# A rarely taken search on VectorE: eight pairs of MAX8 and replacement written out in place of a hardware loop over two pairs

## The chip, the cores and the metric

One core of one Trainium2 chip runs the whole program. The metric is the device time of one execution in microseconds (us), as the median of several runs. Times inside the kernel come from one profiled execution.

## The reference, cut to what matters

A decoder layer runs over 32 sequences of 256 tokens with 512 features: self-attention with 16 heads of 32 features and a gate, then cross-attention, then a mixture of adapter matrices, with a layer norm behind each. The part that matters here is the attention, which keeps for each query and head only the 64 largest of its 256 scores:

```python
scores = jnp.einsum('bhqd,bhkd->bhqk', qn, kn)
temp = jax.nn.sigmoid(x.mean(axis=1) @ Wt + bt) + 0.5
scores = scores / temp[:, None, None, :]
kk = max(1, S // 4)
vals, idx = jax.lax.top_k(scores, kk)
w = jax.nn.softmax(vals, axis=-1)
...
out = jnp.einsum('bhqk,bhkd->bhqd', attn, v)
```

## The kernel before

The work is cut by sequence (called a batch here), and within one by `s`, of which there are four: 128 queries by 8 heads. Every engine has a hand-written order of steps, the function `body`, in which three sequences overlap: the front of sequence i+1, the attention of i and the end of i-1. On PE, ACT and POOL the bodies follow one another as straight code. On VectorE (DVE) two bodies, for an even and an odd sequence, stand inside a hardware loop (lines 2051 to 2054). The loop is run 14 times and covers sequences 2 to 29; sequences 0, 1, 30 and 31 have bodies of their own, so there are six bodies with attention in the code.

Per `s`, the threshold of each row is not found by a full sort. A guess is made from the moments of the row, ACT subtracts it while it copies the scores (`copy_scores`, L789) and counts signs (L809), and DVE looks at the 16 scores nearest to the guess (`search`, L1824 to L1835) and picks the threshold (`set_threshold`). A head in which some row cannot be settled in this way is doubtful. PE and ACT count them, and DVE reads the count into a register in `keep_top` (L1863).

`keep_top` then has two ways. If no head of the eight is doubtful, eight instructions of `keep_above` (L1867) mask the probabilities with the threshold and sum them. Otherwise the code of the `Else` part makes a mask of the doubtful heads in a register and goes through the heads one by one: a settled head gets `keep_above`, a doubtful one gets `keep_struck`, which strikes the eight largest scores of every row eight times over (`strike`: MAX8, L1873, and a replacement, L1874), and keeps what was struck (L1883). Both ways end at the reciprocal `kept_inv` (L1905), for which POOL waits to scale the probabilities (L523) and ACT to copy the next scores into the buffer that comes free (L789).

Each `strike` waits on the semaphore `slow` after both of its instructions. `Steps.restart` (L51 to L56) waits until the count is reached and clears the semaphore. In the kernel before, this is done in every pass of the loop over two strikes. The call site of both ways is:

```python
with dve.If(n < 1):
    for k in range(HS):
        keep_above(k)
with dve.Else():
...
    for k in range(HS):
        step.n = before + k
        with dve.If((doubtful & 2 ** k) > 0):
            keep_struck(k)
```

The `Else` part stands in the code behind the eight `keep_above`, so that the usual way jumps over it (the unconditional branch of L1887).

Of the kernel before, what the change touches and what calls it, by code (L numbers as in the profile page):

```python
# [31 lines left out]
def at(batch, per_batch, n):  # L32

    return batch * per_batch + n
# [24 lines left out]
def decoder_layer(nc, x, ctx, aWq, abq, aWk, abk, aWv, abv, aWo, abo, aWt, abt, aWg, abg,  # L59
# [12 lines left out]
    ROUNDS = KEEP // 8  # L72
# [4 lines left out]
    with stack:  # L77
# [1632 lines left out]
        def _(dve):  # L1710
            step = Steps(dve, s_dve)
            slow = Steps(dve, s_slow)
# [143 lines left out]
            def keep_top(b, s):  # L1856

                r = s % 2
                dve.wait_ge(s_th, at(b, NS, s + 1))
                dve.wait_ge(s_ex, at(b, NS * NH, NH * s + NH))  # L1860
                dve.wait_ge(s_fl, at(b, NS, s + 1))
                dve.sem_inc(s_seq_v, 1)
                n = dve.value_load(unsure_n[0:1, r, HS:HS + 1].bitcast(I32), min_val=0, max_val=MOST)  # L1863
                before = step.n
                def keep_above(k):
                    h, j = divmod(k, HQ)
                    step.mark(dve.scalar_tensor_tensor(  # L1867
                        out=probs[:, r, h, j], in0=scores[:, r, h, j], scalar=threshold[:, r, k:k + 1],
                        in1=probs[:, r, h, j], op0=ALU.is_ge, op1=ALU.mult, accum_out=kept_sum[:, r, k:k + 1]))

                def strike(k):
                    h, j = divmod(k, HQ)
                    slow.wait(slow.mark(dve.max(top8[:], scores[:, r, h, j])))  # L1873
                    slow.wait(slow.mark(dve.match_replace(scores[:, r, h, j], top8[:], scores[:, r, h, j], STRUCK)))  # L1874

                def keep_struck(k):

                    h, j = divmod(k, HQ)
                    with dve.Fori(0, ROUNDS // 2):
                        strike(k)  # L1880
                        strike(k)
                        slow.restart()
                    step.mark(dve.scalar_tensor_tensor(  # L1883
                        out=probs[:, r, h, j], in0=scores[:, r, h, j], scalar=STRUCK / 2,
                        in1=probs[:, r, h, j], op0=ALU.is_le, op1=ALU.mult, accum_out=kept_sum[:, r, k:k + 1]))
# [5 lines that stand above are left out]
                    slow.wait(slow.mark(dve.scalar_tensor_tensor(  # L1891
                        out=head_bits[:, 0:HS], in0=unsure_n[:, r, 0:HS], scalar=0.0, in1=bit_weights[:],
                        op0=ALU.is_gt, op1=ALU.mult, accum_out=head_bits[:, HS:HS + 1])))
                    slow.mark(dve.tensor_copy(head_mask[:], head_bits[:, HS:HS + 1]))
                    slow.restart()
                    doubtful = dve.value_load(head_mask[0:1, 0:1], min_val=0, max_val=2 ** HS - 1)
# [7 lines that stand above are left out]
                step.wait(step.n)  # L1904
                dve.reciprocal(kept_inv[:, r], kept_sum[:, r]).then_inc(s_inv, 1)  # L1905
# [178 lines left out]
```

## Time and profile before

| what | value |
|---|---|
| median of 3 runs | 3202.72 us (3202.55 to 3206.73) |
| profiled execution, its own time | 3211.29 us |
| span of the profiled execution | 3209.3 us |
| DVE busy | 2729.7 us (85%), 10113 instructions |
| PE busy | 2837.4 us (88%) |
| ACT busy | 2119.9 us (66%) |
| POOL busy | 1583.2 us (49%) |
| mean granted clock of PE | 0.959 of full speed |

The time of the profiled execution runs about 2 us beyond its span. Register, branch and semaphore instructions are handled by an engine's sequencer and are not counted as busy; in the trace they stand under the name of the engine with a q (DVEq). An instruction that replaces (MATCH_REPLACE in the program) is recorded as two, MATCH_VALUE_LOAD and MATCH_REPLACE8, and a SCALAR_TENSOR_TENSOR with a sum as two, itself and DVE_READ_ACCUMULATOR. The packets by which instructions are loaded into the engines stand in the DMA part under "instruction".

### The profile page before, as it was taken

The page shows a single profiled execution, that of the slowest core. Times are in us where ns is not written, and L with a number is a line of the kernel's source. Part 1 is how long each engine was busy: PE and PEld are TensorE (multiplying, and loading weights), DVE is VectorE, ACT ScalarE, POOL GpSimd, SP SyncE. Part 2 cuts the span into 40 slices and gives each one's busy share as a digit, 9 for nine tenths or more (in the row PEclk, how much of TensorE's full clock was granted, in tenths as well). Part 3 has the DMA queues.
Part 4 walks back from the last instruction along what each step waited for, and adds up shares of the span by engine and source line. Part 5 has one row for each costly group of instructions (what it writes and reads, how often), then busy time and mean ns, then how long its engine had stood idle before and what let it go on. Part 6 is the DMA issues. An engine that isn't in the chain of part 4 may idle for free. (4 is left out here: it accounts for less than half of the span.)

```text
span 3209.3 us, 58791 instructions
## 1 busy us (share of the span) xinstructions
PE 2837.4 (88%) x16154; PEld 1560.3 (49%) x16154; DVE 2729.7 (85%) x10113; ACT 2119.9 (66%) x5970; POOL 1583.2 (49%) x2285
## 2 busy tenths in 40 slices
PE   6799999989899789998998999999988998989755
PEld 4455555545455345554554555555545554545333
DVE  4889889888888898888888898988988898888881
ACT  3577777766576557766766777777767776657541
POOL 3345555545455444554544554555545454545422
PEclk8899999999999989999999999999999999999877
DMA  6000000000000000000000000000000000000000
GB/s 226 8 18 25 25 24 22 19 10 24 24 25 22 5 24 25 25 22 4 25 25 24 25 21 25 17 13 25 25 24 22 24 18 11 24 24 18 9 10 13
DMA packets 43674, 80.04 MB, mean 25 GB/s; under 512 B 3914, under 2 KB 12106, under 8 KB 43186
## 3 DMA queue, kind: packets, MB, share of 16 engines
q1 hardware_dynamic: 41682, 69.18, 6.6%
q0 software_dynamic: 1504, 5.77, 0.5%
q14 instruction: 354, 2.90, 0.3%
q8 instruction: 134, 2.20, 0.3%
HBM read 58.16 MB, written 16.78 MB: 23 GB/s over the span
## 5 line engine op out<-in xcount | busy, mean ns | idle before, releaser
L523 POOL TENSOR_SCALAR probs<-probs,kept_inv 128x256 f32<-128x256 f32 x1024 | 474.0, 486 | 611.0 <-DVE kept_inv L1905 611.0
L789 ACT ACTIVATE scores<-score_ps,neg_guess 128x256 f32<-128x256 f32 x1024 | 397.5, 480 | 233.4 <-DVE kept_inv L1905 197.8
L1867 DVE SCALAR_TENSOR_TENSOR probs<-scores,threshold,probs 128x256 f32<-128x256 f32 x1011 | 434.0, 492 | 137.5 <-ACT unsure_n L815 107.5
L809 ACT ACTIVATE near<-scores 128x256 f32<-128x256 f32 x1024 | 411.3, 415 | 4.2 <-DVE nearest L1834 1.1
L824 ACT ACTIVATE probsT<-work_ps 128x512 f32<-128x512 f32 x512 | 292.7, 597 | 181.0 <-PE work_ps L1122 178.4
L1830 DVE MATCH_REPLACE8 near<-nearest,near 128x256 f32<-128x256 f32 x1024 | 406.8, 407 | 0.0
L1122 PE MATMUL work_ps<-ident,probs 128*128 128x128 f32 x2072 | 324.0, 291 | 79.2 <-POOL probs L523 36.7
L1826 DVE MAX8 nearest<-near 128x8 f32<-128x256 f32 x1024 | 358.1, 410 | 9.8 <-DVE near L1818 8.7
L1834 DVE MAX8 nearest<-near 128x8 f32<-128x256 f32 x1024 | 356.9, 409 | 0.0
L490 POOL TENSOR_TENSOR inv_norm<-sumsq,minus_half 128x32 f32<-128x32 f32 x64 | 351.2, 5488 | 5.3
L1818 DVE TENSOR_SCALAR near<-scores,flip 128x256 int32<-128x256 int32 x1024 | 307.1, 367 | 4.5
L1122 PEld LDWEIGHTS work_ps<-ident,probs 128*128 128x128 f32 x2072 | 231.3, 145 | 156.0 <-issue 68.7
L799 ACT ACTIVATE probs<-score_ps 128x1024 f32<-128x1024 f32 x256 | 260.0, 1034 | 2.0 <-PE work_ps L1122 0.3
L1183 PE MATMUL work_ps<-w_f,rows 128*128 128x512 f32 x512 | 240.6, 613 | 9.9 <-ACT rows L671 9.9
L1183 PE MATMUL work_ps<-w_o,attnT 128*128 128x512 f32 x512 | 238.3, 608 | 0.6 <-ACT attnT L832 0.6
L1183 PE MATMUL work_ps<-w_g,xT 128*128 128x512 f32 x512 | 237.6, 607 | 0.0
L1183 PE MATMUL work_ps<-w_k,xT 128*128 128x512 f32 x512 | 236.4, 605 | 0.9 <-DMA w_k<-in_L_attn_Wk_dram 0.9
L1183 PE MATMUL work_ps<-w_q,xT 128*128 128x512 f32 x512 | 234.3, 601 | 1.2 <-ACT qk L704 1.2
L1183 PE MATMUL work_ps<-w_v,xT 128*128 128x512 f32 x512 | 233.4, 598 | 1.2 <-ACT w_f L665 1.2
L533 POOL TENSOR_SCALAR rstd<-mean_var 128x2 f32<-128x2 f32 x96 | 26.6, 277 | 387.3 <-DVE mean_var L1911 382.8
L1302 PE MATMUL work_ps<-probsT,v_sb 128*32 128x128 f32 x4096 | 148.9, 285 | 69.4 <-DVE sq L1787 66.6
L1128 PEld LDWEIGHTS work_ps<-bias_rows,ones_rows 3*128 3x128 bf16 x448 | 40.6, 91 | 340.5 <-issue 340.5
(173 smaller groups left out, 5484.0 us busy)
## 6 DMA issues: line engine op xcount, KB each, us to landing
x_in<-in_x_dram SPq DMA_DIRECT2D x32, 512.0 KB, 3.7
x_res<-in_x_dram SPq DMA_DIRECT2D x32, 512.0 KB, 3.6
out_dram<-rows SPq DMA_DIRECT2D x32, 512.0 KB, 3.0
c_sb<-in_ctx_dram SPq DMA_DIRECT2D x32, 256.0 KB, 2.7
rows<-in_L_ffn_W_dram SPq DMA_DIRECT2D x8, 512.0 KB, 4.7
gate_t<-in_L_ffn_W_dram SPq DMA_DIRECT2D x3, 512.0 KB, 3.7
v_sb<-in_L_ffn_W_dram SPq DMA_DIRECT2D x3, 512.0 KB, 4.5
w_q<-in_L_attn_Wq_dram POOLq DMA_DIRECT2D x1, 1024.0 KB, 8.9
```

The costliest lines, as they stand in the source:

```text
L490: step.wait(step.mark(pool.tensor_tensor(inv_norm[:, t], sumsq[:, t], minus_half[:, 0:2 * H], ALU.pow)))
L523: pool.tensor_scalar(probs[:, s % 2, h, j], probs[:, s % 2, h, j], kept_inv[:, s % 2, n:n + 1], 1.0, ALU.mult, ALU.mult).then_inc(s_pr, 1)
L789: last = act.activation(scores[:, s % 2, h, j], score_ps[:, j, h], ACT.Identity, bias=neg_guess[:, t, n:n + 1])
L809: last = act.activation(near[:, h, j], scores[:, s % 2, h, j], ACT.Sign, accum_out=sign_sum[:, s % 2, n:n + 1])
L824: act.activation(probsT[:, h, 2 * a:2 * a + 2], W[BANK_TP[s][2 * h + a]][:].rearrange("p (h k n) -> p h k n", h=2, k=NT), ACT.Copy).then_i ...
L1122: last = pe.transpose(dst[:, n * P:n * P + P], part, ident[:])
L1183: pe.matmul(dst, src[:, kt, t * P:t * P + P], w[:, kt], start=kt == 0, stop=False)
L1818: last = dve.tensor_scalar(near[:, h, j].bitcast(I32), scores[:, r, h, j].bitcast(I32), flip[:, r, n:n + 1].bitcast(I32), None, ALU.bitwis ...
L1826: c = [step.mark(dve.max(nearest[:, h * HQ + j, 0:8], near[:, h, j])) for j in range(HQ)]
L1830: d.append(step.mark(dve.match_replace(near[:, h, j], nearest[:, h * HQ + j, 0:8], near[:, h, j], STRUCK)))
L1834: last = dve.max(nearest[:, h * HQ + j, 8:16], near[:, h, j])
L1867: step.mark(dve.scalar_tensor_tensor(out=probs[:, r, h, j], in0=scores[:, r, h, j], scalar=threshold[:, r, k:k + 1], in1=probs[:, r, h, j] ...
```

## The change

`keep_struck` has its eight strikes one behind the other, with one restart at the end, in place of four passes over two strikes with a restart in each. The whole diff is:

```diff
-                    with dve.Fori(0, ROUNDS // 2):
+                    for _ in range(ROUNDS):
                         strike(k)
-                        strike(k)
-                        slow.restart()
+                    slow.restart()
```

`ROUNDS` is 8. The strikes that a doubtful head executes are the same 8 as before. The function is expanded for 8 heads in each of 24 `keep_top` (4 in each of six bodies), so the code that is written out grows. On DVE, in the code of `keep_struck` and of the settled way behind it, for one head of a `keep_top`, before:

```order
L1899 COMPARE_AND_BRANCH
L1879 UNCONDITIONAL_BRANCH
L1873 MAX top<-scores 128x8
L1874 MATCH_REPLACE scores<-top,scores 128x256
L1873 MAX top<-scores 128x8
L1874 MATCH_REPLACE scores<-top,scores 128x256
L55 ISA
L1879 REGISTER_ALU
L1879 COMPARE_AND_BRANCH
L1883 SCALAR_TENSOR_TENSOR probs,kept_sum<-scores,probs 128x256
L1899 UNCONDITIONAL_BRANCH
```

ISA of L55 is the clearing of the semaphore; the second COMPARE_AND_BRANCH goes back to the first MAX. The same place after the change, from the seventh of the eight pairs on (the lines behind L1878 have moved up by one):

```order
L1873 MAX top<-scores 128x8
L1874 MATCH_REPLACE scores<-top,scores 128x256
L1873 MAX top<-scores 128x8
L1874 MATCH_REPLACE scores<-top,scores 128x256
L55 ISA
L1882 SCALAR_TENSOR_TENSOR probs,kept_sum<-scores,probs 128x256
L1898 UNCONDITIONAL_BRANCH
```

The counter and the branch of the loop are gone, and six more pairs stand ahead of these. The program of DVE has 3603 such rows before and 5331 after; those of the other engines are unchanged.

## Rows read from the trace of the kernel before

**Rows 1.** The page, busy time (share of the span) and instructions of each engine.
```profile
PE 2837.4 (88%) x16154; PEld 1560.3 (49%) x16154; DVE 2729.7 (85%) x10113; ACT 2119.9 (66%) x5970; POOL 1583.2 (49%) x2285
```

**Rows 2.** What DVE waited for: us in total, times, longest us.
```profile
DVE probs L1867 <- ACT unsure_n L815: 107.5, 54, 4.0
DVE sumsq L1777 <- issue: 39.5, 13, 3.2
DVE top L1873 <- DVE scores L1874: 18.9, 39, 0.6
DVE kept_inv L1905 <- DVE probs L1867: 2.7, 9, 0.7
```

**Rows 3.** Line 1905, who waited for it: us, times.
```profile
  POOL probs L523: 611.0, 97
  ACT scores L789: 197.8, 33
```

**Rows 4.** Four turns of DVE's loop: window, length, DVE busy, granted clock, DMA.
```profile
458.47:640.21 181.74, 162.44 (x608) 1.00 0.07 22
847.27:1028.72 181.45, 162.35 (x608) 1.00 0.07 22
1426.79:1621.46 194.67, 170.42 (x635) 0.96 0.06 20
1621.46:1816.04 194.58, 170.42 (x635) 0.96 0.06 21
```

**Rows 5.** Timeline of DVE, a doubtful head: start us, us, instruction [idle before].
```profile
709.28 0.43 DVE L1873 MAX8 top<-scores 128x8 f32<-128x256 f32 x1 [1.00 <-DVE head_mask L1894]
...
710.26 0.43 DVE L1873 MAX8 top<-scores 128x8 f32<-128x256 f32 x1
...
711.70 0.43 DVE L1873 MAX8 top<-scores 128x8 f32<-128x256 f32 x1 [0.49 <-DVE scores L1874]
...
718.04 0.41 DVE L1874 MATCH_REPLACE8 scores<-top,scores 128x256 f32<-128x256 f32 x1
718.81 0.43 DVE L1883 SCALAR_TENSOR_TENSOR probs<-scores,probs 128x256 f32<-128x256 f32 x1 [0.36 <-DVE scores L1874]
```

**Rows 6.** Lines 1883, 1879 and 1887: instructions, duration ns min/median/max, first and last start.
```profile
L1883 DVE SCALAR_TENSOR_TENSOR probs<-scores,probs x13: 424/426/426, 718.8 to 3101.8; 128x256 f32<-128x256 f32 x13
L1879 DVEq ALU_OP  x52: 40/40/45, 711.4 to 3101.6; - x52
L1887 DVEq COMPARE_BRANCH  x244: 43/53/73, 103.3 to 3133.2; - x122
```

**Rows 7.** DMA queues of the page: packets, MB, share of 16 engines.
```profile
q14 instruction: 354, 2.90, 0.3%
q8 instruction: 134, 2.20, 0.3%
```

**Rows 8.** Line 2051 around 458 us, the branch back of the loop.
```profile
L2051 DVEq COMPARE_BRANCH  x1: 73/73/73, 458.5 to 458.5; - x1
```

**Rows 9.** A jump of L1887 at 512 us, and DVE behind it.
```profile
L1887 DVEq COMPARE_BRANCH  x1: 47/47/47, 512.0 to 512.0; - x1
...
514.34 0.09 DVE L1867 DVE_READ_ACCUMULATOR probs<-scores,threshold,probs 128x1 f32 x1
514.46 0.20 DVE L1905 RECIPROCAL kept_inv<-kept_sum 128x8 f32<-128x8 f32 x1
```

**Rows 10.** The jump at 602.6 us: branch; DMA from 602.5 to 606 in 40 slices; DVE.
```profile
L1887 DVEq COMPARE_BRANCH  x1: 53/53/53, 602.6 to 602.6; - x1
...
GB/s 0 0 0 0 0 0 0 94 0 0 0 0 0 0 0 0 0 0 0 0 0 0 0 0 0 0 0 0 0 0 0 0 0 0 0 0 94 0 0 0
...
604.89 0.09 DVE L1867 DVE_READ_ACCUMULATOR probs<-scores,threshold,probs 128x1 f32 x1
605.11 0.20 DVE L1905 RECIPROCAL kept_inv<-kept_sum 128x8 f32<-128x8 f32 x1
```

**Rows 11.** What DVE waited for, 458.4 to 2946 us (13 turns of its loop).
```profile
DVE kept_inv L1905 <- DVE probs L1867: 1.5, 6, 0.3
```

## The prediction

> **What bounds the kernel now.** I read the page's busy times first, then what DVE waits for, then who waits for the step that the change touches, then single turns of DVE's loop. PE is busy for 88% of the span and DVE for 85% [rows 1], so neither share settles it. The waits say more: DVE waits for ACT's count of doubtful heads 107.5 us in all, and it loses 39.5 us in 13 waits that have no releaser, each at the first instruction of a turn of its loop [rows 2]. In the other direction POOL stands idle 611 us and ACT 197.8 us until `kept_inv` [rows 3]. DVE is thus the engine that others follow around `keep_top`.
>
> The turns show how much of a delay there reaches the end. Two turns without a doubtful head take 181.74 and 181.45 us, and two with one such head each take 194.67 and 194.58 [rows 4], 13.0 us more. A doubtful head by itself takes about 10 us on DVE, from 709.28 to its last mask at 718.81 and that mask's 0.4 us [rows 5]; the mask of heads in a register (its first MAX8 waited 1.00 us for it) comes on top. So nothing of the delay is hidden; the granted clock of PE even goes from 1.00 to 0.96 in such a turn, where PE has stood idle meanwhile. I take a microsecond saved or lost on DVE in `keep_top` as a microsecond at the end.
>
> **What the change removes.** The trace has 13 doubtful heads and 52 passes of the loop, four per head [rows 6]. Within a pass, one MAX8 follows the last after 710.26 - 709.28 = 0.98 us. Over the loop's edge it takes 711.70 - 710.26 = 1.44 us [rows 5]. Three such edges per head become plain pairs: 3 x (1.44 - 0.98) = 1.38 us. At the last edge the mask comes 718.81 - (718.04 + 0.41) = 0.36 us behind the replacement. The wait and the clearing stay there, and the counter (0.04 us, [rows 6]) and the branch, of about the same length, go, with the sequencer's steps between them: I take 0.16 of the 0.36 us. The move that loads the counter ahead of the loop, about 0.05 us, goes too. Together 1.6 us per head, and 13 x 1.6 = **20.7 us** saved.
>
> The Trainium skill, page "Advanced Engine Details and Errata", section "Control Flow Timing", gives a compare-and-branch about 108 ns. An estimate from that page for 52 of them would be 5.6 us saved; the edge in the trace costs 0.46 us because the branch comes behind a semaphore wait, the clearing and the counter, with the next MAX8 dispatched only after it, and I go by the trace.
>
> **What it adds: code that is jumped over.** The settled way was taken 244 - 128 = 116 times of 128 (each of the 128 `keep_top` has one compare, and each settled one a branch at its end, all on L1887, [rows 6]). That branch jumps over the whole `Else` part. Counted in recorded instructions, one head was 18: the two that test it, the move, six for two pairs, the wait, the clearing, counter and branch, two for the mask, the branch out, and two for `keep_above`. It becomes 33: 24 for eight pairs, and three fewer for the loop. With 7 ahead of the heads the jump goes over 7 + 8 x 18 = 151 before and 7 + 8 x 33 = 271 after.
>
> Instructions are loaded in packets. Queue 8 moved 2.20 MB in 134 of them, which fits PE with its 2 x 16154 matmuls and weight loads and some 2000 other instructions at 64 B each; queue 14, for the other engines, has packets of 2.90 MB / 354 = 8 KB [rows 1, 7], or 128 instructions. So the jump spanned 1.2 such pieces and will span 2.1. Before, it ended in the very next piece from 104 of 128 starting points, and after, never: from 112 points it ends two pieces on, else three.
>
> What a jump to a piece that isn't there costs can be seen at two places. The loop's branch back is at 458.5 us [rows 8], and the first instruction of the next turn comes 3.0 us late on the average (39.5 / 13, [rows 2]). The forward jump at 602.6 us is followed by a packet 0.6 us later (slice 8 of 40 in 3.5 us) and a second at 605.7, and the reciprocal starts at 605.11, 0.13 us behind the sum that ended at 604.98 [rows 10]. At 512 us the same jump leaves the usual 0.03 us (514.43 to 514.46) [rows 9]. The reason why a stall of about 2.5 us costs only 0.1 us is that the eight masks have already been handed to DVE when its sequencer jumps: 2.4 us of work lie between the branch at 512.0 and the end of the last sum. This cover is what I rest on; where it is gone, a jump costs the full 3 us of the branch back.
>
> The price per long jump is then bounded from below by 0, where the cover is longer, and from above by 3.0 - 2.4 = 0.6 us, if a forward jump is as slow as the branch back. In 13 turns of the loop the waits of the reciprocal add up to 1.5 us [rows 11]. By the count of positions one of the eight jumps in a turn is a long one there, the one at 602.6 us and its likes, so that one costs 1.5 / 13 = 0.12 us. This is the nearest row, the same jump over about the same code, and I take it. Before, some 16 of the 116 were long, after, all are: 100 x 0.12 = 12 us, less 1.5 us for two before the loop and one behind it that cost more by falling on the edge of a piece (2.7 - 1.5 = 1.2 us in three waits, [rows 2, 11]), and less about 1 us for jumps with a longer cover. I put **9.5 us** added, with 0 and 60 us as the ends.
>
> **The doubtful way itself** is entered 12 times. It now runs through 271 instructions, and its settled heads take 0.41 us each while they use up 33 instructions: four of them, 1.6 us, use up a piece, and a piece takes about 2.4 us to follow (the two packets of [rows 10] are 2.5 us apart). A second piece within a row of settled heads can thus be 0.8 us late. Where the struck head lies between, its 8 us cover it. With part of it covered by queued masks I take 0.25 us x 12 = **3 us** added, between 0 and 10.
>
> **Sum.** -20.7 + 9.5 + 3 = -8.2 us against the profiled execution's own 3211.3 us, or 3203.1. That execution lies 8.6 us above the median shown, which runs without the profiler; the difference of versions should be the same there: 3202.7 - 8.2 = **3194.5 us**. About 0.2% (6.4 us) is what a measurement of this kernel can tell from no change.
>
> **Rivals.** First, **slower through late code**: each long jump costs not 0.12 us but what the nine waits that the profile names cost on the average, 2.7 / 9 = 0.3 us [rows 2], since jumps of three pieces, or ones that land shortly ahead of the end of one, wait longer. That is 100 x 0.3 - 2.7 = 27 us added, and with 3 and -20.7 us the time is 3212. It decides as soon as the mean price passes 0.2 us. For it speaks that all but one of the long jumps seen inside the loop are of one place; against it, that this place was passed 13 times and gave 0.3 us at the most. At its upper end, 0.6 us per jump, the time would be 3240.
>
> Second, **no cost of code at all**: the window holds the landing place anyway, and only the saving is left, 3202.7 - 20.7 = 3182 us. The packets of 8 KB and the second packet behind the jump at 602.6 us speak against it [rows 7, 10]. The Trainium skill, page "Runtime: NRT & Kernel Launch", section "Instruction fetch mechanics", says that an engine other than PE holds two blocks of 16 KiB, 256 instructions each, and that a taken branch out of them stalls for a fetch. By that page a jump over 271 instructions would leave the two blocks from 16 of 256 starting points only; the trace agrees with a fetch behind a jump but shows half that block.
>
> Third, **even**: the jumps cost about 0.2 us each (20 us added less the 2.7), or half of the saving is lost elsewhere, for instance because PE, whose busy share is above DVE's [rows 1], sets the pace in part of a turn. The time stays within 6 us of before.
>
> **How the numbers follow.** I give the forecast 0.40, late code 0.25, no cost 0.13, even 0.22. Of the forecast's share about a fifth lies above -6.4 us. Faster by over 0.2% is then 0.32 + 0.13 = 0.45; within it 0.08 + 0.22 = 0.30; slower 0.25. The range goes down to 3180 (the second rival with the granted clock a little better), and up to 3215, past the first rival's price, so that its worse half and little else is outside.
>
> **What would show it.** Between two MAX8 of a doubtful head 0.98 us throughout, no wait named between them, and such a head at about 8.4 us in place of 10. Turns of DVE's loop without a doubtful head longer by about 0.8 us (seven more long jumps of 0.12), with one shorter by about 0.5 (1.6 less 0.8 and 0.25). The waits of the reciprocal for the last sum at some 12 us in place of 2.7, in many more than 9 places, and more packets on queue 14. The waits at the head of a turn stay at 3 us. I am wrong if turns without a doubtful head grow by over 2 us, or not at all.

## The result, and the profile after

| | before | after |
|---|---|---|
| median | 3204.72 us (4 runs, 3202.55 to 3207.09) | 3264.64 us (4 runs, 3263.34 to 3269.89) |
| span of the profiled execution | 3209.3 us | 3261.7 us |
| mean granted clock of PE | 0.959 | 0.958 |

The ratio is 1.0188, with an interval of 1.0174 to 1.0202: the changed kernel is 60 us slower. The forecast was 8 us faster, with a range that ended at 3215. Size and sign are both wrong.

From the page of the changed kernel come the busy times (us, share of the span, instructions) and the two queues of instruction packets (packets, MB, share of 16 engines):

```profile
PE 2850.3 (87%) x16154; PEld 1569.3 (48%) x16154; DVE 2729.7 (84%) x10113; ACT 2119.6 (65%) x5970; POOL 1587.8 (49%) x2285
...
q14 instruction: 479, 3.92, 0.4%
q8 instruction: 134, 2.20, 0.3%
```

DVE does the same work to the tenth of a microsecond [rows 1], so all 52.4 us between the two spans are idle time on it. Queue 14 brings 125 packets more [rows 7], queue 8 none. What DVE waited for in the changed kernel (us in total, times, longest us; "issue" is a wait for which the profile has no releaser):

```profile
DVE probs L1867 <- ACT unsure_n L815: 79.6, 41, 3.3
DVE probs L1867 <- issue: 65.2, 59, 2.5
DVE kept_inv L1904 <- DVE probs L1867: 42.3, 85, 1.0
DVE sumsq L1777 <- issue: 41.2, 13, 3.7
DVE kept_inv L1904 <- issue: 28.4, 23, 1.4
...
DVE flip L1806 <- ACT near L809: 19.8, 31, 1.4
DVE near L1830 <- issue: 9.3, 11, 1.1
...
DVE rows L1919 <- issue: 6.7, 14, 0.5
```

The wait of the reciprocal was 2.7 us in 9 places [rows 2] and is 42.3 + 28.4 = 70.7 us in 108. A wait inside the search (L1830, 9.3 us) is new. The 18.9 us that a MAX8 waited at the loop's edges [rows 2] are gone. `rows` L1919 has a new wait of 6.7 us in 14 places. The waits at L1867 as a whole, those on `head_mask` included, grow from 136.1 us to 149.0; most of what is new in its "issue" row stood under ACT's count before. POOL and ACT follow, as the row of who waited for L1904 shows (us, times), against 611.0 and 197.8 us [rows 3]:

```profile
  POOL probs L523: 637.7, 97
  ACT scores L789: 208.2, 37
```

Turns of DVE's loop in the changed kernel (window, length, DVE busy and instructions, granted clock, DMA), two without a doubtful head and two with one:

```profile
859.83:1047.23 187.40, 162.38 (x608) 0.99 0.07 22
1263.03:1450.46 187.43, 162.37 (x608) 0.99 0.07 22
1450.46:1648.76 198.30, 170.31 (x635) 0.97 0.07 20
1648.76:1846.60 197.84, 170.32 (x636) 0.97 0.07 21
```

A turn without a doubtful head grew by about 6 us, one with such a head by 3.4 [rows 4]. Call a turn without a doubtful head clean. The mean over all clean turns (six of 13) goes from 181.65 to 187.69 us. The 13 turns together took 2486.6 us and take 2540.9, which is 54.3 more; what lies ahead of them grew by 1.3 and what lies behind shrank by 3.2. The 54.3 us are 13 x 6.04 = 78.5 of growth, less 24 us by which the seven turns with doubtful heads (ten heads) grew less. Some 8 of these 24 are saved in the ten doubtful ways themselves; the rest isn't broken down.

Where the 6.0 us of a clean turn lie can be read from DVE's idle time, as means over the six clean turns, before and after. The eight reciprocals wait 0.4 and 5.0 us, L1830 0 and 0.9, L1919 0.1 and 0.5, and the first mask of each of the eight `keep_top` (L1867) 8.3 and 9.2 in all. The wait for ACT at `flip` (L1806) falls from 2.4 to 1.3, and all else grows by 0.2. The sum is 19.2 us of idle time before and 25.1 after. So small stalls beside the reciprocals count too, and a part of all of them is hidden where DVE would have waited for ACT anyway.

The doubtful head itself does what the change says. Timeline of DVE in the changed kernel (start us, us, instruction, idle before):

```profile
722.10 0.43 DVE L1873 MAX8 top<-scores 128x8 f32<-128x256 f32 x1 [0.92 <-DVE head_mask L1893]
...
723.09 0.43 DVE L1873 MAX8 top<-scores 128x8 f32<-128x256 f32 x1
...
729.54 0.41 DVE L1874 MATCH_REPLACE8 scores<-top,scores 128x256 f32<-128x256 f32 x1
730.15 0.43 DVE L1882 SCALAR_TENSOR_TENSOR probs<-scores,probs 128x256 f32<-128x256 f32 x1 [0.21 <-DVE scores L1874]
```

The pitch of 0.98 us holds through all eight pairs, and from the first MAX8 to the mask it is 8.05 us where it was 9.53 [rows 5]: 1.48 us per head, 1.6 predicted. Over the 13 heads that is 104.6 us in place of 124.2, so 19.6 saved. Not all of it is left at the end of the way: from the first instruction of a doubtful way (`head_bits`) to the end of its reciprocal the 12 ways take 186.4 us before and 176.2 after, only 10.2 less. The masks of settled heads within these ways wait 22.1 us in place of 13.0, which is the late code of the way itself.

**An ordinary jump.** The settled way now jumps over 271 recorded instructions every time. Here is the branch of L1886 in the changed kernel (durations ns, first and last start us), then the DMA of 2197.5 to 2201.5 in 40 slices of 0.1 us, then DVE:

```profile
L1886 DVEq COMPARE_BRANCH  x1: 47/47/47, 2197.8 to 2197.8; - x1
...
GB/s 0 0 0 0 0 0 0 0 0 0 0 0 82 0 0 0 0 0 0 0 0 0 0 0 0 0 0 0 0 0 0 0 0 0 0 0 0 0 82 0
...
2200.69 0.20 DVE L1904 RECIPROCAL kept_inv<-kept_sum 128x8 f32<-128x8 f32 x1 [0.52 <-DVE probs L1867]
```

The packet comes 0.9 to 1.0 us behind the branch, not 0.6 us as at 602.6 us [rows 10], and the reciprocal starts 2.9 us behind it. The eight masks cover 2.4 us of that, and 0.5 us is exposed. Most ordinary jumps are like this. In some the packet comes later, 1.1 to 1.3 us behind the branch, and then the reciprocal starts 3.0 us behind it and waits 0.6 us (17 such jumps in this trace, against 65 with the packet at 0.9 to 1.1).

**A jump from just ahead of the end of a piece.** The same three views at 2039.65 us, DMA from 2039.6 to 2043.6:

```profile
L1886 DVEq COMPARE_BRANCH  x1: 53/53/53, 2039.7 to 2039.7; - x1
...
GB/s 0 0 0 0 0 0 0 0 82 0 0 0 0 82 0 0 0 0 0 0 0 0 0 0 0 0 0 0 0 164 0 0 0 0 0 0 0 0 0 0
...
2043.32 0.20 DVE L1904 RECIPROCAL kept_inv<-kept_sum 128x8 f32<-128x8 f32 x1 [1.20 <-issue]
```

There are two packets of 8 KB, 0.7 to 0.8 and 1.2 to 1.3 us behind the branch (the third, of 16 KB, is on queue 8), and the reciprocal comes 1.2 us late. Counted from the start of the code, this jump leaves from instruction 123 or 124 of a piece of 128. My reading is that the sequencer had already asked for the piece after next when it jumped; the jump ends one further on, and its packet comes second. Two of the eight jumps in a turn stand so; their reciprocals wait 1.3 and 1.1 us, means of six turns. How far the sequencer reads ahead is inferred from the times of packets, not recorded.

**A landing just ahead of the end of a piece.** Timeline of DVE in the changed kernel:

```profile
2092.94 0.07 DVE L1830 MATCH_VALUE_LOAD near<-nearest,near 128x8 f32 x1
2094.04 0.42 DVE L1830 MATCH_REPLACE8 near<-nearest,near 128x256 f32<-128x256 f32 x1 [1.01 <-issue]
```

This is shortly behind the place where a jump lands. The trace has seven instructions from the landing to here; my count puts the landing 12 ahead of the end of a piece, so the next piece would begin close by, and the trace alone doesn't settle the exact place. The stall of 1.0 us (0.9 on the average of six turns) stands between the two halves of one replacement, where no semaphore and no data are waited for. Counted over the recorded instructions of a turn, two more grown waits stand within two instructions of the same place in a piece: L1919, 0.5 us in place of 0.1, and the first mask of one `s`, 2.4 us in place of 2.1. Both are absent in after50 below.

### The profile page after: what moved, and what is told of

Same layout as the page of the kernel before. It is cut to its first block and busy times, and to the rows that moved or that the text cites. A ratio compares the mean times of both kernels' runs of the same rounds, so it can differ in the third digit from the quotient of the medians.

```text
span 3261.7 us, 58596 instructions
## 1 busy us (share of the span) xinstructions
PE 2850.3 (87%) x16154; PEld 1569.3 (48%) x16154; DVE 2729.7 (84%) x10113; ACT 2119.6 (65%) x5970; POOL 1587.8 (49%) x2285
## 3 DMA queue, kind: packets, MB, share of 16 engines
q14 instruction: 479, 3.92, 0.4%
## 5 line engine op out<-in xcount | busy, mean ns | idle before, releaser
L1867 DVE SCALAR_TENSOR_TENSOR probs<-scores,threshold,probs 128x256 f32<-128x256 f32 x1011 | 435.3, 492 | 150.3 <-ACT unsure_n L815 79.6
L1830 DVE MATCH_REPLACE8 near<-nearest,near 128x256 f32<-128x256 f32 x1024 | 407.1, 408 | 9.3 <-issue 9.3
L809 ACT ACTIVATION_READ_ACCUMULATOR near<-scores 128x1 f32 x1024 | 205.8, 201 | 0.0
```

The source lines that it names most:

```text
L809: last = act.activation(near[:, h, j], scores[:, s % 2, h, j], ACT.Sign, accum_out=sign_sum[:, s % 2, n:n + 1])
L1830: d.append(step.mark(dve.match_replace(near[:, h, j], nearest[:, h * HQ + j, 0:8], near[:, h, j], STRUCK)))
L1867: step.mark(dve.scalar_tensor_tensor(out=probs[:, r, h, j], in0=scores[:, r, h, j], scalar=threshold[:, r, k:k + 1], in1=probs[:, r, h, j] ...
```

## The experiments

Each ratio is to the kernel before, run again beside the experiments (medians of 3205.5 to 3206.8 us).

The first group asks whether the unexecuted code costs the time, where it stands, and whether other work can cover the jump.

**dead118.** The kernel before, its loops kept, with a block behind the eight heads that is never entered:

```diff
+                    with dve.If((doubtful & 2 ** HS) > 0):
+                        for _ in range(118):
+                            dve.memset(top8[:, 0:1], 0.0)
```

> The kernel before, with its loop over two pairs kept, and 118 memsets that are never executed behind the eight heads of the Else part (with the test ahead of them 120 instructions), so that the settled way jumps over 271 instructions as in the changed kernel. Theory (the jump is what costs: its landing place is never among the two 8 KB pieces that DVE's sequencer holds): a turn of DVE's loop without a doubtful head takes 187.4 us as in the changed kernel, against 181.6 before, and the total is the changed kernel's 3264.6 plus the 20.7 us of loop edges that are kept: 3285 us. Rival (the straight pairs themselves cost, or what the doubtful way does): turns stay at 181.6 us and the total at 3205.

Measured: 3205.19 us, ratio 0.9996 (0.9986 to 1.0006), with 354 packets on queue 14 as before [rows 7]. The register is declared to be below 2 ** HS, and the build left the block out: this was the kernel before once more. It says nothing of the theories, only how well one program repeats.

**after50.** The changed kernel with its code moved by 50 instructions, which run once at the start:

```diff
             def setup():
+                for _ in range(50):
+                    dve.sem_inc(s_seq_v, 1)
                 dve.wait_ge(s_const, NCONST)
```

> The changed kernel with 50 more semaphore increments at the start of DVE's program, which move all of its later code by 50 instructions. By my count of positions the two jumps that stood 4 and 5 instructions ahead of the end of a piece (late by 1.1 to 1.4 us each) now stand 45 and 46 into one, no jump is left near an end, and no landing is within 18 of one. Theory: every jump costs the ordinary 0.5 us, 7 x 0.52 = 3.6 us per turn, so that a turn without a doubtful head takes 185.2 us in place of 187.4, and the total is 14 x 2.2 = 31 us less, 3234 us. Rival (position does not matter, only the amount of code): 3264 us, turns at 187.4.

Measured: 3222.23 us, ratio 1.0055 (1.0039 to 1.0072). Where the same instructions begin within their pieces is worth 42 us of the 60, more than any theory gave it. The waits of DVE in after50 have one row for the reciprocal, without the "issue" row beside it and with none at L1830; the turn (columns as above) is in the second fence:

```profile
DVE kept_inv L1906 <- DVE probs L1869: 51.0, 104, 1.0
```
```profile
2008.90:2192.15 183.25, 162.60 (x609) 1.00 0.07 22
```

On the average a reciprocal waits 51.0 / 104 = 0.49 us. That is the ordinary price of a long jump, four times my 0.12. By place in a clean turn the averages are 0.44 to 0.47 us for six of the jumps, 0.13 for one with a longer cover, and 0.73 for one that has an additional packet 0.2 us behind its branch and its own only at 1.1. The mean clean turn is 184.25 us: of the 6.0 us of growth, 3.4 came from the edges of pieces (the two jumps, the landing, and the smaller waits at L1919 and at first masks), and 2.6 from all the jumps being long.

**shift48.** The kernel before with 48 such increments.

```diff
             def setup():
+                for _ in range(48):
+                    dve.sem_inc(s_seq_v, 1)
```

> The kernel before with 48 more semaphore increments at the start of DVE's program. By my count two of the eight jumps of a turn become long ones at ordinary places (107 and 116 of 128), and one stays long from 123, like the one at 602.6 us in the kernel before, only another one. Theory: turns without a doubtful head grow from 181.6 by 2 x 0.5 = 1.0 us to 182.6, the total by 14 us to 3218; the reciprocal waits at three places of a turn, two at 0.4 to 0.6 us and one at about 0.1. Rival (a long jump costs 0.12 us wherever it is, and something else made the changed kernel slow): turns at 181.9, total 3208.

Measured: 3219.7 us, ratio 1.0046 (1.0029 to 1.0062). The reciprocal's wait in shift48:

```profile
DVE kept_inv L1907 <- DVE probs L1869: 17.2, 42, 0.7
```

With the old code length, moving it makes the reciprocal wait in more than four times as many places (42 waits, 0.41 us each, against 9). A clean turn takes 182.34 us on the average, 0.7 more than before, and the 13 turns together 2497.7 us, 11.1 more; the turns with doubtful heads grew by more than the clean ones (7.0 us in seven turns). Outside the loop nothing was added. The spans of the profiled executions are 10.5 us apart; the last 4 of the 14 us between the medians I can't place. One of the jumps here is long and cheap (packet 0.6 us behind the branch, wait under 0.1 us), and it leaves from five instructions ahead of the end of its piece for the piece after next. That is the place of the jump at 602.6 us [rows 10] again.

**tail.** The changed kernel with the reciprocal and the DVE work behind it written into both ways, so that the jump comes later, with that work queued:

```diff
                 with dve.If(n < 1):
                     for k in range(HS):
                         keep_above(k)
+                    step.wait(step.n)
+                    dve.reciprocal(kept_inv[:, r], kept_sum[:, r]).then_inc(s_inv, 1)
+                    tail()
...
+                    step.n = before + HS
+                    step.wait(step.n)
+                    dve.reciprocal(kept_inv[:, r], kept_sum[:, r]).then_inc(s_inv, 1)
+                    tail()
```

> The changed kernel with the reciprocal and the DVE work that follows each keep_top (key sums and search; statistics and turning; search; statistics) written into both ways, so that the settled way jumps only when this work has also been handed to DVE. The jump is as long as in the changed kernel, or longer by some 20 instructions. Theory (a jump costs what is left of 2.9 us behind the work already handed over): the cover grows by 1.5 to 4 us, nothing is late, turns without a doubtful head are back at 181.6 us and the total is the kernel before less the loop edges, 3204.7 - 20.7 + 3 = 3187 us. Rival (the sequencer's lost time comes back later whatever is queued): turns stay at 185 us or more, total above 3240.

Measured: 3357.78 us, ratio 1.0477 (1.0459 to 1.0494). The reciprocals are on time, and yet it is the slowest of all. The waits of DVE in tail show four new rows, at the first instructions behind each jump:

```profile
DVE flip L1806 <- issue: 74.7, 27, 3.0
DVE t_small L1770 <- issue: 53.4, 30, 2.0
DVE nearest L1826 <- issue: 52.0, 30, 2.0
...
DVE sq L1787 <- issue: 39.7, 25, 1.8
```

One of them by the branch, then the timeline of DVE:

```profile
L1886 DVEq COMPARE_BRANCH  x1: 51/51/51, 2100.0 to 2100.0; - x1
...
2099.87 1.40 DVE L1834 MAX8 nearest<-near 128x8 f32<-128x256 f32 x4
2103.22 0.15 DVE L1770 TENSOR_SCALAR t_small<-t_small 128x1 f32<-128x1 f32 x1 [1.95 <-issue]
```

The sequencer reaches the branch only 0.13 us after the first of the last four MAX8 has started. It seems to go no further than an instruction whose wait isn't met, and the MAX8 wait for the replacements. So 1.4 us of work is queued when it jumps at 2100.0, and the next instruction comes 3.2 us later. That rule is my reading of this timeline. The new layout also moved and lengthened the code that is jumped over, and this run doesn't tell that apart from the lost cover. No cover that was tried was better than eight masks with nothing to wait for.

The second group keeps the loops and adds code that really stays, and shortens it.

**dead119** and **dead239.** The kernel before with the block of dead118 under a condition that the build keeps and that never holds, 119 or 239 instructions long:

```diff
+                    with dve.If(n > 0x7E000000):
+                        for _ in range(119):
+                            dve.memset(top8[:, 0:1], 0.0)
```

> As dead118 was meant: the kernel before, with its loop over two pairs kept, and 119 memsets behind the eight heads of the Else part, under a test of the count of doubtful heads that is never true but that the compiler cannot decide. The settled way jumps over 271 instructions, and all code stands at the positions of the changed kernel. Theory (the jump costs): turns of DVE's loop without a doubtful head take 187.4 us as in the changed kernel, the total is 3264.6 + 20.7 = 3285 us, and queue 14 has the changed kernel's 479 packets. Rival (the straight pairs cost): turns 181.6 us, total 3205.

> The same with 239 memsets: the jump goes over 391 instructions, 3.06 pieces. Theory (a jump out of the two pieces costs the same however far it goes): the same price per ordinary jump, 0.5 us, so turns of 186 to 188 us by where jumps stand, and 3275 to 3290 us in all. Rival (the price grows with the distance): another 6 us per turn, turns at 193, total above 3350.

Measured: dead119 3295.69 us, ratio 1.0277 (1.026 to 1.0295); dead239 3259.76 us, ratio 1.0162 (1.0139 to 1.0185). A turn of each (columns as above), and the reciprocal's waits of each:

```profile
2040.95:2228.13 187.18, 162.87 (x608) 0.99 0.07 22
```
```profile
2027.66:2212.33 184.67, 162.54 (x608) 0.99 0.07 22
```
```profile
DVE kept_inv L1908 <- DVE probs L1867: 38.1, 81, 1.0
DVE kept_inv L1908 <- issue: 31.6, 26, 1.9
```
```profile
DVE kept_inv L1908 <- DVE probs L1867: 46.2, 102, 0.7
DVE kept_inv L1908 <- issue: 28.2, 12, 2.6
```

dead119 has the jump length and the positions of the changed kernel, and nothing of it is ever executed. Its clean turn is near the changed kernel's (186.9 against 187.7 on the average, 181.65 before), with 479 packets on queue 14 like it. Code that never runs is shown to cost the time, 5.3 of the 6.0 us. The changed kernel is 31 us faster than dead119 by the medians and 23.4 by the profiled spans (3285.1 - 3261.7). This is more than the straight pairs save: the doubtful ways of dead119 jump over the dead block too, with little queued to cover it. From `head_bits` to the end of the reciprocal the 12 ways take 195.2 us in it, 8.8 more than in the kernel before, and 6.5 us of reciprocal waits are among them. dead239 jumps over 391 instructions, a piece more, and its clean turn is 3.5 us shorter than dead119's (183.4 on the average). The price of an ordinary jump there is 46.2 / 102 = 0.45 us. It doesn't grow with the distance; what sets it is where the jump starts and ends. The 28.2 us in 12 places are the ends of the 12 doubtful ways, which jump over the dead block with little queued: there the reciprocal waits 2.35 us on the average.

**two_passes.** The kernel before with four pairs in a pass in place of two, so that there are two passes:

```diff
-                    with dve.Fori(0, ROUNDS // 2):
-                        strike(k)
-                        strike(k)
+                    with dve.Fori(0, ROUNDS // 4):
+                        for _ in range(4):
+                            strike(k)
                         slow.restart()
```

> The kernel before with two passes over four pairs. The jump goes over 7 + 8 x 24 = 199 instructions. By my count of positions (59, 116, 20, 20, 69, 123, 27, 27 for the eight jumps of a turn) four are long: two at ordinary places (0.5 us each), one with the longer cover (0.15), one from 123, where the piece that is fetched ahead is the right one (0.1). Theory: turns 181.6 - 0.1 + 1.25 = 182.8 us, 14 x 1.2 = 17 us more, less two loop edges of 0.46 us for each of 13 heads, 12 us: 3210 us. Rival (cost in proportion to the added code, 48 of 120 instructions): turns 183.9, total 3205 + 32 - 12 = 3225.

Measured: 3202.35 us, ratio 0.9991 (0.9981 to 1.0). The reciprocal's wait and a turn:

```profile
DVE kept_inv L1905 <- DVE probs L1867: 14.2, 35, 0.7
```
```profile
1993.07:2175.04 181.97, 162.61 (x608) 1.00 0.07 22
```

This keeps part of the saving and pays for few long jumps. The waits of the reciprocal grow by 11.5 us, and a clean turn by 0.5 on the average (182.17).

**turns.** The kernel before with the outer loop of DVE written out, which removes its 13 branches back:

```diff
-            with dve.Fori(1, B // 2 - 1) as k:
+            for k in range(1, B // 2 - 1):
```

> The kernel before with the 14 turns of DVE's outer loop written out, as the other engines have them, and the loop over two pairs kept. Theory: the 13 waits of 3.0 us behind the branch back vanish, and of the jumps of L1887 the same 19% are long as chance has it, 1.5 in two bodies in place of 1 cheap one, 0.5 us more: 3204.7 - 13 x 3.0 + 14 x 0.5 = 3173 us. Rival (the wait behind the branch back is hidden by waits that follow it): 3205 us or up to 10 less.

Measured: 3204.12 us, ratio 0.9993 (0.9983 to 1.0002). The 39.5 us of [rows 2] are gone, and only about 2 us come of it. What DVE waited for in turns:

```profile
DVE neg_max L1931 <- ACT rows L862: 76.5, 31, 13.1
...
DVE kept_inv L1905 <- DVE probs L1867: 8.5, 20, 0.7
```

The wait for ACT at `neg_max` was 44.6 us in 18 places before and takes up 32 us of it. Two sequences still take 181.7 us on the average (181.5 to 182.1). A clean turn of the kernel before is thus within a few tenths of what the other engines allow (PE is busy for 171 of 180 us), and DVE's 3 us at the loop's head were hidden.

The third group closes what was open: the cover once more, the two causes together, and a version that beats both.

**fill26.** The changed kernel, moved by 26 increments, with a MAX8 of no use queued behind the eight masks in both ways, ahead of the jump:

```diff
                     for k in range(HS):
                         keep_above(k)
+                    step.mark(dve.max(top8[:], scores[:, r, 0, 0]))
```

> after50 with one more MAX8 (result unused, waits for nothing) behind the eight masks in both ways, ahead of the jump, and 26 in place of 50 increments at the start so that all jumps and landings stand at ordinary places again. Theory (the sequencer's 2.9 us run from the branch, and DVE idles for what is left of them behind the work already handed over): the added MAX8, 0.33 us, fills idle time, the reciprocal starts as before relative to the branch, its waits fall from 51 us in all to 15 to 20, and turns stay at 184.3 us (total 3222). Rival (the delay is a fixed addition behind the last mask): the waits stay at 51 us and turns grow by 8 x 0.33 = 2.6 us to 186.9, total 3255.

Measured: 3275.03 us, ratio 1.0211 (1.0194 to 1.0228). First mask, branch, and end of the work in fill26, and the reciprocal's row among its waits:

```profile
L1888 DVEq COMPARE_BRANCH  x2: 50/50/51, 2044.4 to 2045.8; - x2
...
2044.48 0.48 DVE L1869 SCALAR_TENSOR_TENSOR probs<-scores,threshold,probs 128x256 f32<-128x256 f32 x1
...
2047.73 0.42 DVE L1891 MAX8 top<-scores 128x8 f32<-128x256 f32 x1
2048.81 0.20 DVE L1908 RECIPROCAL kept_inv<-kept_sum 128x8 f32<-128x8 f32 x1 [0.66 <-DVE top L1891]
```
```profile
DVE kept_inv L1908 <- DVE top L1891: 52.5, 102, 0.9
```

In after50 the branch starts 0.9 us behind the first mask (2014.8 and 2013.87), in fill26 1.3 us behind it (2045.8 and 2044.48). Over all settled jumps the medians are 0.95 and 1.33 us, and from the branch to the reciprocal it is 2.8 us in both. One more instruction ahead of the branch makes the branch later by about the time of one mask, and 0.5 us per jump stays exposed (52.5 / 102). The added MAX8 thus covers nothing, and the mean clean turn grows from 184.25 to 187.4 us. So the work that is queued at the jump has a limit, of some five operations behind the one running, and the masks already reach it.

**after_turns.** The changed kernel with the outer loop written out in the same way as in turns.

> The changed kernel with DVE's outer loop written out. In the kernel before this removed the 13 waits of 3 us and gave under 2 us in all, each turn stayed at 181.5. Theory A (DVE has some 3 us of slack per turn at one place, the rest is set by PE and ACT; in the changed kernel this slack is used up elsewhere): the turns now fall by less than the 3 us too, as the slack is at another place than the jumps: by 0 to 1 us, plus what the changed positions give (no fixed jump from the end of a piece any more, 1 to 2 us), 3235 to 3255. Theory B (the slack is one sum over the turn, and the jumps ate it up): the full 3 us per turn come back, with the positions 4 to 5, about 3264.6 - 14 x 4.5 = 3202 us.

Measured: 3216.76 us, ratio 1.0027 (1.0016 to 1.0039). In straight code the positions differ from turn to turn, so the bad ones aren't met 13 times over. The waits of the reciprocal:

```profile
DVE kept_inv L1904 <- DVE probs L1867: 42.4, 84, 1.0
DVE kept_inv L1904 <- issue: 7.0, 6, 1.4
```

The "issue" row falls from 28.4 us to 7.0, and two sequences take 183.4 us. This fits after50: with few or no stalls at the edges of pieces the change costs 10 to 17 us, with them met in every turn 60.

**two14.** two_passes with 14 increments at the start of `setup`, to free one more jump of its wait.

> The kernel with two passes over four pairs, and 14 increments at the start of DVE's program. By my count two of the eight jumps of a turn are long in place of four, both of them the first of their body (one with the longer cover). Theory: turns without a doubtful head fall from 182.17 to 181.8 us, the total by 5 us to 3197, so that it beats the kernel before by 8 us. Rival (positions make no difference here): 3202.

Measured: 3202.16 us, ratio 0.9985 (0.9976 to 0.9995). The reciprocal's waits in two14:

```profile
DVE kept_inv L1907 <- DVE probs L1869: 7.7, 18, 0.6
```

They fall from 14.2 to 7.7 us, and the total shows no gain that can be told from two_passes. Four of the six clean turns take 181.8 to 182.1 us and two 183.5 and 183.9, so their mean, 182.5, is no shorter either. In those two the first mask of one `s` waits 0.65 us where it waits for nothing in the others, and `flip` behind it waits longer for ACT.

**two_turns.** two_passes and the outer loop written out.

> Two passes over four pairs, with DVE's outer loop written out. A bit over half of the jumps are long at ordinary places, 4.5 per two bodies, 0.4 us each, part of it hidden as in the other kernels. Theory A (the slack of the branch back is at another place): two bodies take 182.5 us, total 3203. Theory B (slack is one sum): 181.5 us, and with the 12 us of loop edges 3193.

Measured: 3201.01 us, ratio 0.9981 (0.9971 to 0.999). It is the fastest that was run, 0.2% below the kernel before and 64 us below the changed one. Its reciprocal waits are no shorter:

```profile
DVE kept_inv L1905 <- DVE probs L1867: 21.8, 53, 0.7
```

Each half of it alone gave 0.0007 to 0.0009, so it is at the edge of what can be measured.

## Why the prediction was wrong

**What failed is the price of a long jump: "In 13 turns of the loop the waits of the reciprocal add up to 1.5 us ... 1.5 / 13 = 0.12 us. This is the nearest row."** The term was 100 x 0.12 = 12 us, put at 9.5 (the 1.5 us taken off for three waits should have been the 1.2 that is worked out beside it). In its place the waits at the reciprocal grew by 70.7 - 2.7 = 68 us, and L1830 and L1919 added 9.3 and 6.7. The row was one place passed 13 times, and it was a special one: a jump from about five instructions ahead of the end of a piece to the piece after next, which had already been asked for. The profile said so, had I read it: its packet came 0.6 us behind the branch and reached the next piece early, while I took 0.6 us for the time of any packet. The three dearer waits outside the loop (1.2 us) were set aside as falling on the edge of a piece; those were the sample of what other places cost. after50 gives 0.49 us for the plain case.

**The second half of the error was that a price per jump doesn't exist.** I computed that all 116 jumps would be long and not where the eight of a turn would stand. Two leave from instruction 123 or 124 of 128 and cost 1.3 and 1.1 us, one landing costs 0.9 us behind it, and plain passages over an edge some tenths (L1919, a first mask); in a hardware loop they are met 13 times. Moving the code away from such places was worth 42 us of the 60 (after50). "Landing shortly ahead of the end" stood in the first rival as a reason, without a price.

**The bound from above, 0.6 us per jump, was too low.** It took the first instruction of a turn to be 3.0 us late and subtracted the cover. Plain jumps keep to it on the average (0.47 to 0.54 us by place in the changed kernel, single ones up to 0.67), those near an edge don't. The first rival had the right mechanism, but its 27 us and even its upper end (3240) are below 3264.64.

**"A microsecond lost on DVE in `keep_top` is a microsecond at the end"** holds for the 10 us of a doubtful head, and no evidence of mine reached further. turns removes 39.5 us and gains about 2; two14 takes 6.5 us from the reciprocal's waits and gains nothing. In after50 the reciprocals of a clean turn wait 3.2 us more than before, and the turn grows by 2.6. In the changed kernel the reciprocals wait 4.7 us more and L1830, L1919 and the first masks 2.1, together 6.8, of which 1.1 come back at `flip`, and the turn grows by 6.0. So a part of the delay is hidden in both. This error was on the safe side and didn't save the sum.

**The doubtful way was mis-sized too.** Its late code was put at 3 us, with 10 as the end. The masks of settled heads in the 12 ways wait 9.1 us more (22.1 against 13.0), so that half of what the straight pairs save is lost again before the way ends.

**Right:** the saving of the straight pairs (20.7 us predicted, 19.6 measured from the first MAX8 to the mask in 13 heads); the lengths of 151 and 271, and that every settled jump would be long; pieces of 8 KB on queue 14, and more packets there; the head of a turn near 3 us (41.2 / 13 = 3.2). The Trainium skill, page "Runtime: NRT & Kernel Launch", section "Instruction fetch mechanics", makes a taken branch out of the blocks held wait for a fetch; the trace agrees. Its block of 256 instructions is not what this queue moves: 3.92 MB in 479 packets is 8 KB, or 128. The text said that I am wrong if clean turns grow by over 2 us: they grew by 6.0, and the late code that this sentence watched for was the cause.

What stays open: how the time from the branch to the landing (2.8 to 2.9 us) is made up, 16 of the 24 us by which turns with doubtful heads grew less, and the last 4 us of shift48. What is told of the read-ahead is a reading of packet times that four kernels fit, not a record of the sequencer.

## What to carry to other kernels

Unrolling a rarely taken way lengthens the code that the usual way jumps over, and that is paid on every usual pass: here 1.5 us was saved in each of 13 places and 0.5 to 1.3 us lost in about 100. Look for a jump's price in several places of the trace and by its position in the pieces of code, because one cheap place in a hardware loop is one sample however often it is passed. A dead block of the same length, or some increments at the start that shift the code, tells the cost of layout apart from the cost of instructions; make sure that the block is still in what was built.

## What the runs showed of the hardware

- Behind a forward jump out of the pieces held, DVE's packet mostly comes 0.9 to 1.1 us after the branch and the next instruction 2.8 to 2.9 us after it; where the packet comes at 1.1 to 1.3 us, it is 3.0. Between 271 instructions (after, after50) and 391 (dead239) that doesn't grow. The branch back of the loop costs about 3 us. At the end of the doubtful ways of dead239, with little queued ahead of the jump, 2.35 us stay exposed (28.2 / 12).
- Where code stands in its pieces of 8 KB was worth 42 us of 3265 in one and the same program (after50), and 14 us in the kernel before (shift48), 10.5 by the profiled spans.
- DVE's sequencer had no more than about five operations queued behind the running one when it branched, with nine operations to queue as with eight (fill26), and in tail it branched with only four MAX8 left, the first of them running. The Trainium skill, page "Advanced Engine Details and Errata", section "Engine Queue Depths", gives VectorE's queue a depth of 8. The five here are counted in operations, and the profile records a mask as two; no run shows whether the queue counts it as one or two, so this neither confirms the 8 nor contradicts it.
